# Clearing the padding rows of two sorted token tables chunk by chunk in the attention stages instead of at the start of the expert stages

## The chip, the cores and the metric

The kernel runs on one core of a Trainium2 chip. The metric is the time of one execution in microseconds of device time; three runs of the kernel before are given. The profile is of one further execution. Engines are named as in the profile: PE (matrix products), DVE (vector), ACT (activations), POOL (GpSimd) and SP (which here only issues transfers).

## What is computed

The reference is a two-layer model on x of shape 16 x 512 x 128 (16 sequences, here called chunks, of 512 tokens, width 128), float32. Each of its four parts is followed by a residual sum and a layer norm:

```python
x = layernorm(x + L0_attn(x))   # 16 heads of 64, exponentials of k1, k2, k3 products, cumulative sums over the tokens
x = layernorm(x + L0_ffn(x))    # 8 experts, each token goes to one: relu(x W1 + b1) W2 + b2, times its probability
x = layernorm(x + L1_attn(x))   # softmax attention, 16 heads of 8, with a bias that depends on the distance
x = layernorm(x + L1_ffn(x))    # a shared gated block plus one of 8 gated experts per token, token scaled by a score
```

Which expert a token goes to is the argmax of its 8 routing logits.

## The kernel before

The program has five stages with a barrier of all engines between them (`program`, L1898): the first attention (`attention_one`, L168), the first experts (`experts`, L826, tag b), the second attention (`attention_two`, L1083, tiles named c_), the second experts (`experts`, tag d) and `finish` (L1717, tiles named e_). Within a stage each engine has its own program, and semaphores order them.

**The sorted tables.** While an attention stage runs, it also routes: for each token of a chunk it chooses the expert and a slot, which is the next free row in that expert's region of a table in HBM, and POOL scatters the token rows there by an indirect DMA, four DMAs of 128 rows a chunk. The table is `xs_d` in the first attention (`route_scatter`, L628) and `zs_d` in the second (`scatter`, L1303). It has eight regions of REGION = 16 x 512 + 512 = 8,704 rows of 512 bytes, and behind them, from row SPARE on, one group of 512 spare rows. Before the scatter of chunk b, at most 512 b tokens have been given out, so every slot of chunk b is below row 512 (b + 1) of its region.

**The experts.** The expert stage works through 24 blocks of 512 rows (GROUP). Each expert's tokens are rounded up to whole blocks, so the last block of an expert has rows behind the last token, and blocks that no expert needs read the spare rows. These padding rows are computed like others and must hold finite numbers; nobody reads what comes of them. At the stage's start DVE works out a plan from the counts (L942 to L980): the expert of each block (`expert`, L964, signalled as `plan_ready` 1) and the first row of each block (`row`, L980, `plan_ready` 2), and behind that the rows for the later gather (L986 to L999). The padding is cleared at the same time: POOL sets a tile of zeros (L933) and one of ones (L934, for which the plan's first instruction waits), DVE converts each expert's end to an integer (`fill`, L940), and SP and ACT each load four of the eight ends into a register and issue a DMA of 512 rows of zeros from there on (`fill_behind`, L898); SP also clears the spare rows (L905). Only then does SP wait for the plan, load expert and row into registers (`which`), wait for all nine fills, and issue the first block's tokens (L919) and weights (L920). In the blocks PE transposes the tokens (L1060), ACT copies them out of PSUM, PE multiplies (L1052, L1073) and DVE writes the output tile.

**The order of SP's work in the first attention.** SP's program is a software pipeline over chunks, written out by hand in `step`: at step s it loads the turned x of chunk s + 1 (`load_turned`, L281, once the values of chunk s - 1 are through), the token-wise x of chunk s (`load`, L286, once `y_read` counts s - 1), and stores the normed rows of chunk s - 2 (L291). PE wants the turned x of chunk s + 1 in the middle of step s (`front_logits`, L360 and L363). All this goes through one queue. In step 0 SP also writes the table of position biases to HBM, in step 2 it loads all of it into SBUF:

```python
                    if isinstance(s.b, int) and s.b == 2:
                        sp.wait_ge(sem("bias_out"), 16 * H)
                        sp.dma_start(keep.bias[:], io["bias_d"].rearrange("h p d q -> p h d q")
```

The write is 16 DMAs of 448 KB (L308), the load is one DMA of 7,168 KB (L319). POOL's step ends with the scatter of chunk s - 3; behind it stand the next step's one-hot, rstd and running sums.

**SP in the second attention.** For each chunk SP writes the three bf16 parts of q and k to HBM (`parts_d`, L1240), waits for them and loads them back stacked in six DMAs (`c_kst`, `c_qst`, L1251), loads x1 of a later chunk (L1233) and stores x3 of the chunk before (L1256). A body of PE is 64 tiles: scores (L1348), the turned exponentials (L1357) and the values (L1370). The scores of the next chunk start six tiles before the body's end.

Of the kernel before, what the change touches and what calls it, by code (L numbers as in the profile page):

```python
# [14 lines left out]
I32 = mybir.dt.int32  # L15
# [4 lines left out]
P = 128  # L20
# [146 lines left out]

def attention_one(nc, g, keep):  # L168
# [9 lines left out]
    with ExitStack() as ctx:  # L178
# [91 lines left out]
        with nc.Block() as block:  # L270

            @block.sync
            def _(sp):
# [36 lines left out]
                def step(s, on):  # L310
                    if on[0]:
                        load_turned(s.ahead())
                    if on[1]:
                        load(s)
                    if isinstance(s.b, int) and s.b == 0:
                        make_bias()
                    if isinstance(s.b, int) and s.b == 2:
                        sp.wait_ge(sem("bias_out"), 16 * H)
                        sp.dma_start(keep.bias[:], io["bias_d"].rearrange("h p d q -> p h d q")  # L319
                                     ).then_inc(sem("bias_ready"), 16)  # L320
                    if on[3]:
                        store(s.back(2))

                loop(sp, step, first=0)
                sp.wait_ge(sem("bias_ready"), 16)
# [229 lines left out]
            def _(pool):  # L555
# [68 lines left out]
                def route_scatter(s):  # L624
                    pool.wait_ge(sem("slot_ready"), s.b + 1)
                    apart(pool, sem("pool_passed"))
                    for t in range(T):
                        pool.indirect_dma_start(  # L628
                            out=io["xs_d"], out_offset=bass.IndirectOffsetOnAxis(ap=slot[s.par][:, t:t + 1], axis=0),
                            in_=x1[s.par][:, t, :], in_offset=None).then_inc(sem(f"scat{s.par}"), 16)  # L630
# [195 lines left out]
def experts(nc, g, keep, tag, src, dst, weights, gated):  # L826
# [17 lines left out]
    with ExitStack() as ctx:  # L844
# [6 lines left out]
        zeros = sb("zeros", [P, T, W])  # L851
# [6 lines left out]
        fill = sb("fill", [P, E], I32)  # L858
# [33 lines left out]
        def fill_behind(eng, experts):  # L892

            eng.wait_ge(sem("zeros_ready"), 1)
            eng.wait_ge(sem("fill_ready"), 1)
            for e in experts:
                r = which(eng, fill, e, SPARE - GROUP)
                eng.dma_start(rows_of(src, r), zeros[:]).then_inc(sem("fill_out"), 16)  # L898

        with nc.Block() as block:  # L900

            @block.sync
            def _(sp):
                fill_behind(sp, range(0, E, 2))
                sp.dma_start(rows_of(src, SPARE), zeros[:]).then_inc(sem("fill_out"), 16)  # L905
                sp.wait_ge(sem("plan_ready"), 1)

                def step(s, on):
                    if on[0]:
# [4 lines left out]
                        if isinstance(s.b, int) and s.b == 0:  # L914
                            sp.wait_ge(sem("fill_out"), 16 * E + 16)
# [15 lines left out]
            @block.gpsimd  # L931
            def _(pool):
                nc.gpsimd.memset(zeros[:], 0.0).then_inc(sem("zeros_ready"), 1)  # L933
                nc.gpsimd.memset(ones8[:], 1.0).then_inc(sem("ones8_ready"), 1)  # L934

            @block.vector
            def _(dve):
                v = nc.vector
                own = Own(dve, sem("own"), sem("dve_passed"))
                v.tensor_copy(fill[:], keep.run[:]).then_inc(sem("fill_ready"), 1)  # L940
# [82 lines left out]
            def _(act):  # L1023
                fill_behind(act, range(1, E, 2))

# [57 lines left out]
def attention_two(nc, g, keep):  # L1083
# [36 lines left out]
    with ExitStack() as ctx:  # L1120
# [103 lines left out]
        with nc.Block() as block:  # L1224

            @block.sync
            def _(sp):
# [31 lines left out]
                def body(s, tail=True, front=True):  # L1259
                    if front:  # L1260
                        stack(s.ahead())
                        if not isinstance(s.b, int) or s.b + 2 < NB:
                            load(s.ahead().ahead())
# [5 lines left out]
                load(at(1))  # L1269
                body(at(0), tail=False)  # L1270
# [7 lines left out]
                sp.wait_ge(sem("x3_out"), 16 * NB)  # L1278

            @block.gpsimd  # L1280
            def _(pool):
# [17 lines left out]
                def scatter(s):  # L1299
                    pool.wait_ge(sem("slot_ready"), s.b + 1)  # L1300
                    apart(pool, sem("pool_passed"))
# [645 lines left out]
def _layout(**a):  # L1947
# [33 lines left out]
    out["pos"] = np.broadcast_to(n, (P, N))  # L1981
    rows = np.arange(H * SP_).reshape(-1, P)
# [36 lines left out]
```

## Time and profile before

| | |
|---|---|
| three runs | 2399.13, 2405.56, 2406.78 us; median 2405.56 |
| the profiled execution | 2405.52 us, span from the first to the last instruction 2403.7 us |
| mean granted TensorE clock | 0.937 |
| busy share of the span | PE 84%, DVE 68%, ACT 64%, POOL 33% |
| DMA | 83,432 packets, 164.19 MB, mean 68 GB/s |
| of it SP's queue (q1) | 73,844 packets, 142.35 MB, 18.7% of 16 engines' span |

By the timeline the stages begin near 0, 630, 746, 2109 and 2265 us. Times in the profile are from the span's start. A row of the timeline gives start, duration, engine, line, operation, the tile written and the tiles read, a count where several instructions are merged (the duration is then from the first start to the last end), and in brackets how long the engine had been idle before it and what released it. SPq, ACTq and POOLq are the sequencers, where DMAs are issued: the duration there is that of the issue, not of the transfer.

### The profile page before, as it was taken

What the parts mean: (1) busy time and instruction counts of PE and PEld (TensorE: products, weight loads), DVE (VectorE), ACT (ScalarE), POOL (GpSimd) and SP (SyncE); (2) the same over time, 40 slices, a digit from 0 to 9 for tenths busy, and PEclk for the clock granted to TensorE, in tenths of its full rate; (3) what the DMA queues carried; (4) which work ended last, traced back from release to release, by engine and by line L of the source; (5) the groups of instructions that cost most, each with busy time, mean ns of one, the idle gap of its engine ahead of it and who ended that gap; (6) DMA issues with size and microseconds to landing.
All of it is one profiled execution on the core that took longest, in us unless ns stands there. A gap on an engine that the chain in (4) does not pass through costs nothing. (4 is left out here: it accounts for less than half of the span.)

```text
span 2403.7 us, 49686 instructions
## 1 busy us (share of the span) xinstructions
PE 2024.0 (84%) x14348; PEld 1303.3 (54%) x14348; DVE 1641.9 (68%) x4787; ACT 1534.9 (64%) x3427; POOL 796.7 (33%) x806
## 2 busy tenths in 40 slices
PE   8488878887394699999999999999999999669886
PEld 5256555656273455555555555555555555446553
DVE  6377888787212578878887788787877787533266
ACT  3355655554141688888888888888888888523221
POOL 4467888787101211221122122212220220100166
PEclk9788989899696799999999999999999999879999
DMA  2331110100363202210221022102210220044332
GB/s 73 113 141 35 33 35 32 34 28 30 121 214 114 65 25 65 72 54 26 66 71 54 21 71 72 48 26 72 72 46 28 72 62 7 11 162 164 117 97 88
DMA packets 83432, 164.19 MB, mean 68 GB/s; under 512 B 11428, under 2 KB 39076, under 8 KB 80884
## 3 DMA queue, kind: packets, MB, share of 16 engines
q1 hardware_dynamic: 73844, 142.35, 18.7%
q0 software_dynamic: 8192, 16.79, 2.3%
q8 instruction: 116, 1.90, 0.3%
q10 hardware_dynamic: 1152, 2.10, 0.2%
q14 instruction: 128, 1.05, 0.1%
HBM read 110.23 MB, written 58.31 MB: 70 GB/s over the span
## 5 line engine op out<-in xcount | busy, mean ns | idle before, releaser
L1610 DVE CUSTOM_DVE_ANT_0 c_sums<-c_s,bias 128x512 f32<-128x512 f32 x1024 | 671.9, 686 | 183.1 <-PE c_s L1348 143.7
L1498 ACT ACTIVATE c_sums<-c_sums,c_low 128x512 f32<-128x512 f32 x1024 | 735.3, 743 | 40.0 <-DVE c_low L1610 28.9
L1357 PE MATMUL c_turned<-ident,c_sums 128*128 128x128 f32 x4096 | 635.9, 278 | 28.9 <-ACT c_pT L1205 27.9
L1357 PEld LDWEIGHTS c_turned<-ident,c_sums 128*128 128x128 f32 x4096 | 499.5, 143 | 180.4 <-ACT c_pT L1205 92.2
L1205 ACT COPY c_pT<-c_turned 128x512 f32<-128x512 f32 x768 | 455.6, 593 | 130.1 <-PE c_turned L1357 128.9
L1348 PE MATMUL c_s<-c_kst,c_qst 72*128 72x512 bf16 x1024 | 399.4, 391 | 46.5 <-DMA c_qst<-parts_d 28.2
L1370 PE MATMUL c_o<-c_pT,c_vst 128*32 128x256 f32 x4096 | 328.6, 393 | 0.7 <-ACT c_pT L1205 0.7
L1297 POOL TENSOR_TENSOR c_rstd<-c_ve,minus_half 128x4 f32<-128x4 f32 x32 | 32.9, 1029 | 639.4 <-DVE c_ve L122 639.4
L1205 DVE COPY c_pT<-c_turned 128x512 f32<-128x512 f32 x256 | 176.6, 690 | 87.3 <-PE c_turned L1357 85.1
L1348 PEld LDWEIGHTS c_s<-c_kst,c_qst 72*128 72x128 bf16 x1024 | 102.4, 100 | 233.3 <-issue 125.7
L505 ACT ACTIVATE v<-a_bank,gain 128x64 f32<-128x64 f32 x768 | 166.3, 345 | 55.5 <-DVE vp L718 55.4
L371 PE MATMUL a_bank<-wv,xT 128*128 128x512 f32 x256 | 153.5, 685 | 19.9 <-ACT v L505 15.2
L513 ACT COPY oT<-a_bank 128x512 f32<-128x512 f32 x128 | 69.7, 587 | 148.7 <-PE a_bank L392 148.6
L572 POOL TENSOR_TENSOR q<-q,vp 128x1024 f32<-128x1024 f32 x48 | 122.8, 2558 | 107.3 <-DVE vp L718 107.1
L583 POOL TENSOR_TENSOR s<-q,v 128x1024 f32<-128x1024 f32 x48 | 143.1, 2980 | 0.2
L400 PEld LDWEIGHTS a_bank<-wo,oT 128*128 128x128 f32 x1024 | 130.2, 203 | 14.3 <-issue 14.3
L718 DVE TENSOR_TENSOR vp<-a_bank,ez 128x512 f32<-128x512 f32 x96 | 64.8, 687 | 104.3 <-PE a_bank L371 102.6
L1303 POOL DMA_INDIRECT zs_d<-c_xs,c_slot x64 | 62.9, 982 | 217.4 <-DVE c_slot L1666 200.8
L400 PE MATMUL a_bank<-wo,oT 128*128 128x128 f32 x1024 | 132.4, 286 | 0.0
L1370 PEld LDWEIGHTS c_o<-c_pT,c_vst 128*32 128x32 f32 x4096 | 81.3, 108 | 87.6 <-issue 86.1
L734 DVE TENSOR_TENSOR o<-o,r 128x1024 f32<-128x1024 f32 x64 | 127.9, 2018 | 0.0
L392 PE MATMUL a_bank<-ident,o 128*128 128x128 f32 x512 | 81.6, 310 | 54.2 <-DVE o L734 53.4
(252 smaller groups left out, 2788.9 us busy)
## 6 DMA issues: line engine op xcount, KB each, us to landing
c_kst<-parts_d SPq DMA_DIRECT2D x48, 384.0 KB
c_qst<-parts_d SPq DMA_DIRECT2D x48, 384.0 KB
parts_d<-c_parts SPq DMA_DIRECT2D x32, 384.0 KB, 2.5
d_w<-in_wd SPq DMA_DIRECT2D x24, 384.0 KB, 3.2
b_w<-in_wb SPq DMA_DIRECT2D x24, 321.0 KB, 3.3
bias_d<-line_d SPq DMA_DIRECT2D x16, 448.0 KB
bias<-bias_d SPq DMA_DIRECT2D x1, 7168.0 KB, 21.9
b_x<-xs_d SPq DMA_DIRECT2D x24, 256.0 KB, 2.5
```

Of the source, the lines that this page charges most:

```text
L371: nc.tensor.matmul(v_ps[h][:], xT[s.par][:, t, :], wv[:, 512 * h:512 * h + 512], start=True, stop=True).then_inc(sem("v_ready"), 1)
L400: mm = nc.tensor.matmul(y_ps[:, t * W:(t + 1) * W], oT[t % 2][:, k, :], wo[:, k, :], start=(k == 0), stop=(k == HA // P - 1))
L505: ins = nc.scalar.activation(dst[:, h * A:(h + 1) * A], v_ps[half][:, k * A:(k + 1) * A], ACT.Copy, scale=gain[s.par][:, t, h:h + 1])
L572: nc.gpsimd.tensor_tensor(q[:, t, :], q[:, t - 1, :], vp[t % 2][:], ALU.add).then_inc(sem("q_ready"), 1)
L583: nc.gpsimd.tensor_tensor(s1[s.par][:, t, :], q[:, t - 1, :], v2[t % 2][:], ALU.add).then_inc(sem("s1_ready"), 1)
L734: v.tensor_tensor(heads(o[t % 2][:]), heads(o[t % 2][:]), r[s.par][:, t, :].unsqueeze(2).to_broadcast([P, H, A]), ALU.mult).then_inc(sem(" ...
L1205: engine(pT[r % 2][:, :, m // 2, m % 2 * P:(m % 2 + 1) * P], pT_ps[m % 2][:]).then_inc(sem(copied(s, n)[0]), 1)
L1348: nc.tensor.matmul(s_ps[n % BANKS][:], qst[s.par][:, h, t * P:(t + 1) * P], kst[s.par][:, h, :], start=True, stop=True).then_inc(sem("s_ps ...
L1357: mm = nc.tensor.transpose(pT_ps[n % 2][:, c, :], sums[n % BUFS][:, c * P:(c + 1) * P], keep.ident[:])
L1370: mm = nc.tensor.matmul(o_ps[ARRAY * i:ARRAY * (i + 1), r % 2 * 2 * P:(r % 2 + 1) * 2 * P], vst[s.par][:, c, f:f + ARRAY], pT[r % 2][:, c, ...
L1498: nc.scalar.activation(sums[b][:], sums[b][:], ACT.Exp, bias=low[b][:], scale=-1.0).then_inc(sem("exp_done"), 1)
L1610: v.tensor_tensor_reduce(sums[n % BUFS][:], s_ps[n % BANKS][:], bias, 1.0, 3.0e38, ALU.add, ALU.min, low[n % BUFS][:]).then_inc(sem("low_r ...
```

## The change

Two helpers are added. `clear_rows` is a DMA from a new input of zeros (128 x 2,048 bytes in HBM) to rows 512 b to 512 b + 511 of all eight regions; `clear_spare` clears the spare rows. SP issues `clear_spare` once and one `clear_rows` per chunk in each attention stage: in the first behind the token-wise load of step b, in the second at the start of body b, that is behind the store that ends the body before. POOL's scatter of chunk b first waits until the clears 0 to b have landed, and SP waits for all of them at the stage's end. The first 16 of each region's 17 groups are cleared. In the expert stages the zeros tile, the integer ends, the nine fills and the waits for them are gone. The whole diff (no other line differs):

```diff
@@ -163,6 +163,17 @@
     own.wait()
     own.did(v.tensor_reduce(slotf[:], sel[:], AX, ALU.add))
     own.wait()
+
+
+def clear_rows(eng, name, b, io, done):
+
+    regions = io[name][0:SPARE, :].rearrange("(e r) w -> e r w", e=E)
+    eng.dma_start(regions[:, bass.ds(GROUP * b, GROUP), :].rearrange("e (p t) w -> p e (t w)", t=T),
+                  io["zeros"].unsqueeze(1).to_broadcast([P, E, T * W])).then_inc(done, 16)
+
+
+def clear_spare(eng, name, io, done):
+    eng.dma_start(io[name][bass.ds(SPARE, GROUP), :].rearrange("(p t) w -> p (t w)", t=T), io["zeros"]).then_inc(done, 16)
 
 
 def attention_one(nc, g, keep):
@@ -312,6 +323,7 @@
                         load_turned(s.ahead())
                     if on[1]:
                         load(s)
+                        clear_rows(sp, "xs_d", s.b, io, sem("rows_clear"))
                     if isinstance(s.b, int) and s.b == 0:
                         make_bias()
                     if isinstance(s.b, int) and s.b == 2:
@@ -321,7 +333,10 @@
                     if on[3]:
                         store(s.back(2))
 
+                clear_spare(sp, "xs_d", io, sem("spare_clear"))
                 loop(sp, step, first=0)
+                sp.wait_ge(sem("spare_clear"), 16)
+                sp.wait_ge(sem("rows_clear"), 16 * NB)
                 sp.wait_ge(sem("bias_ready"), 16)
                 sp.wait_ge(sem("x1_out0"), 16 * NB // 2)
                 sp.wait_ge(sem("x1_out1"), 16 * NB // 2)
@@ -623,6 +638,7 @@
 
                 def route_scatter(s):
                     pool.wait_ge(sem("slot_ready"), s.b + 1)
+                    pool.wait_ge(sem("rows_clear"), 16 * (s.b + 1))
                     apart(pool, sem("pool_passed"))
                     for t in range(T):
                         pool.indirect_dma_start(
@@ -848,14 +864,12 @@
         bank = [ctx.enter_context(nc.psum_tensor(f"{tag}_bank{i}", [P, GROUP], F32)) for i in range(8)]
         turn_ps, gate_ps, h_ps = bank[0:2], bank[2:4], bank[4:6]
         y_ps = [b[:].rearrange("p (t w) -> p t w", t=T) for b in bank[6:8]]
-        zeros = sb("zeros", [P, T, W])
         count = sb("count", [P, E])
         blocks = sb("blocks", [P, E])
         ones8 = sb("ones8", [P, E])
         ends = sb("ends", [P, E])
         offs = sb("offs", [P, E])
         first = sb("first", [P, E])
-        fill = sb("fill", [P, E], I32)
         past = sb("past", [P, BLOCKS, E])
         ef = sb("ef", [P, BLOCKS])
         isf = sb("isf", [P, BLOCKS, E])
@@ -889,20 +903,10 @@
         def rows_of(name, first):
             return io[name][bass.ds(first, GROUP), :].rearrange("(p t) w -> p t w", t=T)
 
-        def fill_behind(eng, experts):
-
-            eng.wait_ge(sem("zeros_ready"), 1)
-            eng.wait_ge(sem("fill_ready"), 1)
-            for e in experts:
-                r = which(eng, fill, e, SPARE - GROUP)
-                eng.dma_start(rows_of(src, r), zeros[:]).then_inc(sem("fill_out"), 16)
-
         with nc.Block() as block:
 
             @block.sync
             def _(sp):
-                fill_behind(sp, range(0, E, 2))
-                sp.dma_start(rows_of(src, SPARE), zeros[:]).then_inc(sem("fill_out"), 16)
                 sp.wait_ge(sem("plan_ready"), 1)
 
                 def step(s, on):
@@ -911,8 +915,6 @@
                         if isinstance(s.b, int) and s.b == 0:
                             sp.wait_ge(sem("plan_ready"), 2)
                         r = which(sp, row, s.b, SPARE)
-                        if isinstance(s.b, int) and s.b == 0:
-                            sp.wait_ge(sem("fill_out"), 16 * E + 16)
                         need(sp, sem("y_ps"), s.b - 3)
                         if not gated:
                             need(sp, sem("y_ready"), s.b - 3)
@@ -930,14 +932,12 @@
 
             @block.gpsimd
             def _(pool):
-                nc.gpsimd.memset(zeros[:], 0.0).then_inc(sem("zeros_ready"), 1)
                 nc.gpsimd.memset(ones8[:], 1.0).then_inc(sem("ones8_ready"), 1)
 
             @block.vector
             def _(dve):
                 v = nc.vector
                 own = Own(dve, sem("own"), sem("dve_passed"))
-                v.tensor_copy(fill[:], keep.run[:]).then_inc(sem("fill_ready"), 1)
                 dve.wait_ge(sem("ones8_ready"), 1)
                 own.did(v.tensor_scalar(offs[:], keep.iota[:], float(REGION), None, ALU.mult))
                 own.did(v.tensor_scalar(first[:], keep.iota[:], float(REGION), None, ALU.mult))
@@ -1021,8 +1021,6 @@
 
             @block.scalar
             def _(act):
-                fill_behind(act, range(1, E, 2))
-
                 def step(s, on):
                     if on[0]:
                         act.wait_ge(sem("turn_ps"), s.b + 1)
@@ -1257,6 +1255,7 @@
                                  ).then_inc(sem("x3_out"), 16)
 
                 def body(s, tail=True, front=True):
+                    clear_rows(sp, "zs_d", s.b, io, sem("rows_clear"))
                     if front:
                         stack(s.ahead())
                         if not isinstance(s.b, int) or s.b + 2 < NB:
@@ -1267,6 +1266,7 @@
                 load(at(0))
                 stack(at(0))
                 load(at(1))
+                clear_spare(sp, "zs_d", io, sem("spare_clear"))
                 body(at(0), tail=False)
                 with sp.Fori(0, NB // 2 - 2) as i:
                     for s in steps(i, 2):
@@ -1276,6 +1276,8 @@
                 body(at(NB - 1), front=False)
                 store(at(NB - 1))
                 sp.wait_ge(sem("x3_out"), 16 * NB)
+                sp.wait_ge(sem("spare_clear"), 16)
+                sp.wait_ge(sem("rows_clear"), 16 * NB)
 
             @block.gpsimd
             def _(pool):
@@ -1298,6 +1300,7 @@
 
                 def scatter(s):
                     pool.wait_ge(sem("slot_ready"), s.b + 1)
+                    pool.wait_ge(sem("rows_clear"), 16 * (s.b + 1))
                     apart(pool, sem("pool_passed"))
                     for t in range(T):
                         pool.indirect_dma_start(
@@ -1979,6 +1982,7 @@
     }
     n = np.linspace(0.0, 1.0, N, dtype=f).reshape(P, T).T.reshape(N)
     out["pos"] = np.broadcast_to(n, (P, N))
+    out["zeros"] = np.zeros((P, T * W), f)
     rows = np.arange(H * SP_).reshape(-1, P)
     out["hmask"] = (rows.T[:, :, None] // SP_ == np.arange(H)).astype(f)
     out["ident"] = np.eye(P, dtype=f)
```

## Rows read from the trace of the kernel before

**Rows 1.** The page's first line.

```profile
span 2403.7 us, 49686 instructions
```

**Rows 2.** Windows, both attentions: start:end, length, busy us of each engine, PEclk, DMA share, GB/s.

```profile
48.00:630.00 582.00, 431.48 (x2331) 309.68 (x2330) 414.61 (x898) 303.34 (x1200) 416.77 (x385) 0.88 0.16 53
...
745.00:2109.00 1364.00, 1220.40 (x10176) 740.11 (x10176) 1033.09 (x3417) 1104.74 (x2016) 267.48 (x298) 0.96 0.17 51
```

**Rows 3.** Timeline at the start of the first expert stage, all engines.

```profile
629.88 0.53 POOL L933 MEMSET b_zeros<- 128x512 f32 x1 [7.92 <-POOLq L1913]
629.92 0.51 DVE L940 CAST b_fill<-run 128x8 int32<-128x8 f32 x1 [13.58 <-PEq L1913]
630.35 0.13 POOL L934 MEMSET b_ones<- 128x8 f32 x1
630.51 0.17 DVE L942 TENSOR_SCALAR b_offs<-iota 128x8 f32<-128x8 f32 x1
...
631.53 4.24 SPq L898 DMA_DIRECT2D xs_d<-b_zeros  x4
...
632.67 0.18 DVE L964 TENSOR_SCALAR b_expert<-b_ef 128x24 int32<-128x24 f32 x1
...
634.64 0.18 DVE L980 TENSOR_TENSOR b_row<-b_rowf,b_spare 128x24 int32<-128x24 f32 x1
...
635.81 0.44 SPq L905 DMA_DIRECT2D xs_d<-b_zeros  x1
...
638.71 0.23 DVE L999 TENSOR_TENSOR rows<-slots,b_chosen 128x64 uint32<-128x64 f32 x1
639.21 0.36 SPq L919 DMA_DIRECT2D b_x<-xs_d  x1
...
641.66 1.12 PE L1060 MATMUL b_bank<-ident,b_x 128*128 128x128 f32 x4 [27.09 <-DMA b_x<-xs_d]
```

**Rows 4.** Timeline at the start of the second expert stage.

```profile
2113.80 0.18 DVE L980 TENSOR_TENSOR d_row<-d_rowf,d_spare 128x24 int32<-128x24 f32 x1
...
2118.37 0.35 SPq L919 DMA_DIRECT2D d_x<-zs_d  x1
```

**Rows 5.** Windows: writing the bias table, loading it, the tail of the first stack.

```profile
70.00:80.00 10.00, 6.43 (x11) 2.53 (x10) 4.85 (x7) 5.89 (x28) 5.44 (x3) 0.74 0.50 152
...
148.00:158.00 10.00, 7.60 (x52) 6.01 (x51) 8.47 (x19) 3.90 (x12) 5.79 (x3) 0.96 1.03 403
...
784.00:786.00 2.00, 0.00 (x0) 0.00 (x0) 0.00 (x0) 0.00 (x0) 0.00 (x0) 0.50 0.17 74
```

**Rows 6.** Timeline of SP in the first attention, steps 2 to 4.

```profile
115.55 0.33 SPq L281 DMA_DIRECT2D xT<-in_xT  x1
...
137.51 0.44 SPq L319 DMA_DIRECT2D bias<-bias_d  x1
...
148.91 0.33 SPq L281 DMA_DIRECT2D xT<-in_xT  x1
170.64 0.33 SPq L286 DMA_DIRECT2D xtok<-in_x  x1
...
182.71 0.33 SPq L281 DMA_DIRECT2D xT<-in_xT  x1
```

**Rows 7.** Timeline of PE: the logits of chunk 4 in step 3.

```profile
167.28 0.49 PE L360 MATMUL a_bank<-p,ident 128*128 128x192 f32 x2
```

**Rows 8.** Line L281 between 100 and 200 us: issue to landing of its three DMAs.

```profile
DMA to landing us min/median/max: 2.6/2.6/11.8
```

**Rows 9.** Who waited for whom: in total, times, longest.

```profile
PE c_s L1348 <- DMA c_qst<-parts_d: 28.2, 1, 28.2
```

**Rows 10.** Timeline of SP in the second attention, behind the first stack.

```profile
775.21 0.42 SPq L1233 DMA_DIRECT2D c_x<-x_d  x1
```

**Rows 11.** Windows: end of the second stack (all engines), and score matmuls alone.

```profile
854.00:858.00 4.00, 4.00 (x38) 2.47 (x37) 3.83 (x11) 3.00 (x6) 0.00 (x0) 1.00 0.03 11
...
796.00:870.00 74.00, 26.68 (x65) 0.93 0.18 52
```

## The prediction

> **What bounds the kernel now.** I read the time stage by stage, because the edit touches four of the five stages in different ways. The profiled execution has a span of 2403.7 us [rows 1] and a time of 2405.52 us; the median of the three runs is 2405.56 us, so the sum below, made against 2405.5, holds for the median too. The runs spread over 7.65 us (2399.13 to 2406.78), 0.3% of the time; under that a measurement of this kernel can hardly tell a change from none.
>
> First the windows by stage [rows 2]. In the first attention PE is busy 431 of 582 us and DVE and POOL some 415 each: three engines close together, DMA share 0.16. In the second attention PE is busy 1220 of 1364 us with DMA share 0.17. Neither stage is bound by transfers, so work given to the DMA engines there has room on average, and the question is where a transfer is waited for.
>
> Then the timeline where the first expert stage begins [rows 3]. PE starts its first transpose at 641.66, released by the DMA of the first token block, which SP issued at 639.21. Everything from 629.9 to 641.7 is start-up on one chain. Two things run side by side in it: DVE's plan, whose last wanted result (the row numbers) is written at 634.64 + 0.18 = 634.82, and SP's clearing of the padding, four fills in 4.24 us and one more, ended at 636.25, then two value loads and a short wait. SP, not the plan, sets the start. The other expert stage has the same picture: plan written at 2113.98, first token DMA at 2118.37 [rows 4].
>
> **Removed: the fills in both expert stages.** Three pieces lie on the path.
>
> (a) POOL's memset of the zeros tile (0.53 us) stands ahead of the memset of ones for which DVE's plan waits. Without it the ones are ready at 629.88 + 0.13 = 630.01 and DVE can start at 630.04 (it started 0.03 us after the ones before), not 630.51: 0.47 us. The first DVE instruction took 0.51 us where like ones take 0.17, so 0.34 of it could be a cost of starting that now falls on the plan. I take 0.40, between 0.1 and 0.47.
>
> (b) SP's issue. The cost of one value load: the fill table is ready at 629.92 + 0.51 = 630.43, and SP's first fill starts at 631.53, 1.10 us later. From the four fills: (4.24 - 0.33) / 3 = 1.30 us from one to the next, less 0.33 of issue, 0.97 us. After the change SP loads the expert number at 632.85 (plan, part one [rows 3]), is done with it by 634.0, waits for part two at 634.82 - 0.40 = 634.42, loads the row number in 1.10 us and issues the first token DMA at 635.52. Before it was 639.21: 3.69 us gained. In the other stage: 2113.98 - 0.40 + 1.10 = 2114.68 against 2118.37, 3.69 us.
>
> (c) ACT's four fills run beside SP's, long before the first transpose, for which ACT waits; and the first tokens took 2.45 us from issue to PE behind nine fills of 256 KB, so their traffic held nothing up: nothing.
>
> Behind the first token DMA everything keeps its spacing: weights, second block, PE. What is late next is still SP's two value loads; DVE's remaining plan, which ended at 638.94, ends near 638.5, and the first block needs DVE only behind transpose, copy and first product, later than 640. So the whole stage moves: -7.4 us for both. Bounds: if both value loads only start after part two, (639.21 - 634.72 - 2.20) = 2.3 each, -4.6; with 0.97 and 0.47, 3.9 each, -7.8.
>
> **Added: 16 clears in each attention.** One clears 512 rows in each of eight regions, 8 x 512 x 512 B = 2.10 MB, in 1,024 pieces of 2 KB, HBM to HBM. No row of before has just that. The nearest one is the writing of the bias table from line_d, also HBM to HBM, in 512 B pieces: 152 GB/s at a DMA share of 0.50 [rows 5]. The fastest is the loading of the bias, 403 GB/s at a share of 1.03. So a clear lasts 2.10/0.403 = 5.2 us at best, 13.8 us if 152 GB/s is all that HBM to HBM gives, and 152/0.50 = 304 GB/s, 6.9 us, if a full share scales. I take 6.9: its row is the same kind of copy, and the clear's pieces are larger. The Trainium skill ("DMA: Bandwidth & Descriptors", section "Why a DMA increments its semaphore by 16 and not by 1") says that the slowest dimensions of the two patterns set the number of engines; by it the clear, with 128 outermost, has all 16 and the sum keeps 6.9, not 13.8. The trace agrees so far: the bias table is written with 7 outermost, and its share of 0.50 is near 7/16.
>
> Most clears are covered. In the first attention SP issues one after the token load, as at 170.97, and its next urgent DMA is the turned x at 182.71 [rows 6]: 11.7 us of room, and a turned x is wanted only 18 us after its issue (148.91 to 167.28 for chunk 4, [rows 7]). Steps of 33.4 us (115.55 to 148.91, with 20 us of full DMA in it) and 33.8 us (to 182.71, with almost none) show that full DMA engines alone don't slow the step. Clears 0 and 1 stand on the queue behind the last DMA that PE waits for there.
>
> **One place isn't covered**: chunk 2. There the clear goes onto SP's queue at 137.5, ahead of the 7 MB bias load, and the turned x of chunk 4 is issued behind that at 148.91. It landed 11.8 us later [rows 8], at 160.7, and PE wanted it at 167.28. The room is 6.6 us. A clear of 6.9 us uses it up: +0.3 us; 5.2 us costs nothing; 13.8 us costs 7.2.
>
> The second attention: the stack transfers are waited for once, 28.2 us at its start [rows 9]. The first clear is issued behind them (SP issued the load behind them at 775.21 [rows 10]), so in ring order it can't hold them up; while their tail runs at 74 GB/s on a share of 0.17, most engines are idle and take the clear. Later stacks have ended by 858, and the 65th score matmul, the first that wants the new stack, comes just before 870 [rows 11]: 12 us of room against a clear issued behind the stack. Nothing.
>
> **Waits.** POOL's scatter now waits for the clears up to its chunk; behind it on POOL stand the next step's rstd and running sums, for which DVE and ACT wait. But clear b is issued three steps (100 us) before scatter b in the first attention, a whole body of 64 tiles ahead in the second. What stays is the instruction: 32 times some 0.03 us, at most 1 us; I take 0.5. The waits of SP at the ends are for clears issued long before.
>
> Sum: 2405.5 - 7.4 + 0.3 + 0.5 = **2398.9 us**.
>
> **Rivals.** *A smaller gain.* SP's start is only partly freed (both value loads behind the plan), -4.6, or a start pays back a few tenths here and there: 2405.5 - 4.6 + 0.8 = 2401.7 us. For it: the plan ends only 1.4 us before the last fill. Against: the expert number is ready 2 us ahead of the row numbers.
>
> *A slow clear ahead of the bias load; slower.* The writes of one clear jump between eight regions 4.25 MiB apart; should that run at the tail's 74 GB/s [rows 5], a clear lasts 28 us, the turned x of chunk 4 lands 21.7 us late for PE, and the time is 2405.5 - 7.4 + 21.7 + 0.5 = 2420 us; each step's turned x would then be at the edge too. It decides from a clear of 13.5 us on, where the stall eats the 7 us gained. For it: no row has such a stride. Against: 304 to 403 GB/s wherever enough engines were busy. The Trainium skill (same page, section on latency and other measured facts) tells of HBM copies with a row pitch of 4 MiB at 103 GB/s and 214 when padded off the power of two. By 103 a clear would last 20 us and the time be near 2412; by 214, 9.8 us and 2402. No run here shows either.
>
> **How the numbers follow.** Forecast as worked out 0.55, a smaller gain or a few us back at chunk 4 0.35, slow clear 0.10. The line of 0.3% is at 2398.3, right beside my 2398.9, and the run spread of 7.65 us lies across it: of the first case somewhat over half comes out faster than that line, the second mostly within it. Faster 0.41, same 0.50, slower 0.09. Range: best sum 2397.7 less half the spread, 2394; upward the smaller gain, a clear of up to 11 us and the spread, 2406.
>
> **Right or wrong in the profile after.** The first token DMA 5.6 us after POOL's first memset in the expert stages, not 9.3; first transpose 2.5 us behind; the fills gone. In the first attention PE's logits of chunk 4 without a DMA wait over 1 us, and the turned x of chunk 4 landing by 168. The wait for the first stack still about 28 us. DMA share in the stages up by 16 x 6.9 us. A wait of POOL's scatter for a clear, or a DMA wait at those logits above 7 us, would prove me wrong.

## The result, and the profile after

The changed kernel takes 2393.03 us (median of 16 runs, 2387.75 to 2400.82), the kernel before 2402.47 us in 16 runs beside it (2398.38 to 2406.78). The ratio is 0.9963, 95% interval 0.9954 to 0.9973: faster by 6.5 to 11 us. The forecast was 2398.9 us with a range of 2394 to 2406, so the time fell 1 us below the range. About half of the 5.9 us between forecast and time is the level, the time of the kernel before from which the forecast subtracts: the kernel before, which I had at 2405.5 us from three runs and one profile, is at 2402.5 us in sixteen.

The profiled execution took 2393.4 us. First the timeline where the expert stages begin, against [rows 3, 4]:

```profile
626.63 0.10 POOL L935 MEMSET b_ones<- 128x8 f32 x1 [7.93 <-POOLq L1916]
626.77 0.17 DVE L942 TENSOR_SCALAR b_offs<-iota 128x8 f32<-128x8 f32 x1 [13.70 <-POOL b_ones L935]
...
628.93 0.18 DVE L964 TENSOR_SCALAR b_expert<-b_ef 128x24 int32<-128x24 f32 x1
...
630.91 0.18 DVE L980 TENSOR_TENSOR b_row<-b_rowf,b_spare 128x24 int32<-128x24 f32 x1
...
631.87 0.36 SPq L921 DMA_DIRECT2D b_x<-xs_d  x1
...
634.58 1.12 PE L1058 MATMUL b_bank<-ident,b_x 128*128 128x128 f32 x4 [23.28 <-DMA b_x<-xs_d]
...
2100.68 0.10 POOL L935 MEMSET d_ones<- 128x8 f32 x1 [3.80 <-POOLq L1916]
...
2104.96 0.18 DVE L980 TENSOR_TENSOR d_row<-d_rowf,d_spare 128x24 int32<-128x24 f32 x1
...
2105.93 0.35 SPq L921 DMA_DIRECT2D d_x<-zs_d  x1
...
2108.44 1.11 PE L1058 MATMUL d_bank<-ident,d_x 128*128 128x128 f32 x4 [19.51 <-DMA d_x<-zs_d]
```

Read each stage from POOL's first memset, since the start itself moves: the first attention was 3.2 us shorter in this execution. To the first token DMA it is 631.87 - 626.63 = 5.24 us, where it was 639.21 - 629.88 = 9.33: 4.09 us gained. In the other stage it is 5.25 us, where it was 2118.37 - 2109.05 = 9.32; the memset of before stands at

```profile
2109.05 0.53 POOL L933 MEMSET d_zeros<- 128x512 f32 x1 [3.83 <-POOLq L1913]
```

The row numbers are ready at 631.09 and SP issues 0.78 us later; the plan, no longer the fills, sets the start.

Then SP's queue in steps 2 and 3 of the first attention, against [rows 6]; PE's logits of chunk 4, against [rows 7]; and the bias load's time to landing from the page (it was 21.9 us):

```profile
137.24 0.33 SPq L297 DMA_DIRECT2D xtok<-in_x  x1
137.61 0.62 SPq L171 DMA_DIRECT2D xs_d<-in_zeros  x1
138.28 0.67 SPq L331 DMA_DIRECT2D bias<-bias_d  x1
147.38 6.91 SPq L302 DMA_DIRECT2D x_d<-x  x1
154.33 1.09 SPq L292 DMA_DIRECT2D xT<-in_xT  x1
170.76 0.33 SPq L297 DMA_DIRECT2D xtok<-in_x  x1
171.13 0.59 SPq L171 DMA_DIRECT2D xs_d<-in_zeros  x1
```

```profile
168.09 0.59 PE L375 MATMUL a_bank<-p,ident 128*128 128x192 f32 x2 [0.53 <-DMA xT<-in_xT]
```

```profile
bias<-bias_d SPq DMA_DIRECT2D x1, 7168.0 KB, 28.5
```

The clear ahead of it made the bias load land 6.6 us later, and PE waits 0.53 us for the turned x: the one uncovered place, near the forecast size of 0.3. The turned x landed 13.7 us behind its issue, at 168.0, at the edge of what I had said; no wait of POOL's scatter for a clear is in the trace. SP's issue of the x1 store took 6.91 us there, of which below.

Last, windows over both attentions [rows 2] and over the clear of chunk 0, and the wait for the first stack [rows 9]:

```profile
48.00:626.60 578.60, 427.77 (x2331) 306.44 (x2330) 413.04 (x897) 301.95 (x1200) 417.42 (x384) 0.89 0.32 108
738.00:2100.00 1362.00, 1218.30 (x10176) 738.68 (x10176) 1034.72 (x3417) 1103.75 (x2016) 266.92 (x298) 0.96 0.24 76
...
17.00:20.00 3.00, 3.00 (x14) 2.84 (x15) 2.93 (x5) 1.26 (x2) 2.27 (x3) 1.00 1.03 401
```

```profile
PE c_s L1351 <- DMA c_qst<-parts_d: 27.5, 1, 27.5
```

DMA share rose from 0.16 to 0.32 and from 0.17 to 0.24, no engine's busy time changed by as much as 1%, and the first stack is waited for as before. From 17 to 20 us, where the kernel before moved nothing, the clear of chunk 0 runs alone at 401 GB/s. The Trainium skill ("DMA: Bandwidth & Descriptors", section "Latency and other measured facts") gives 214 GB/s as the full rate of its HBM-to-HBM copies, and 103 at a pitch of 4 MiB; with regions 4.25 MiB apart this trace shows neither. By the Trainium skill (same page, section "Why a DMA increments its semaphore by 16 and not by 1") the clear uses 16 engines, and the share of 1.03 agrees.

### The profile page after: what moved, and what is told of

The parts are those of the page before. It is cut to its first block and busy times, and to the rows that moved or that the text cites. A ratio compares the mean times of both kernels' runs of the same rounds, so it can differ in the third digit from the quotient of the medians.

```text
span 2391.6 us, 49680 instructions
## 1 busy us (share of the span) xinstructions
PE 2020.0 (84%) x14348; PEld 1300.1 (54%) x14348; DVE 1641.1 (69%) x4785; ACT 1533.0 (64%) x3427; POOL 797.4 (33%) x804
## 5 line engine op out<-in xcount | busy, mean ns | idle before, releaser
L587 POOL TENSOR_TENSOR q<-q,vp 128x1024 f32<-128x1024 f32 x48 | 124.9, 2602 | 104.4 <-DVE vp L734 104.0
L598 POOL TENSOR_TENSOR s<-q,v 128x1024 f32<-128x1024 f32 x48 | 142.9, 2978 | 0.1
L415 PEld LDWEIGHTS a_bank<-wo,oT 128*128 128x128 f32 x1024 | 127.3, 200 | 14.3 <-issue 14.3
L415 PE MATMUL a_bank<-wo,oT 128*128 128x128 f32 x1024 | 129.6, 282 | 0.0
L750 DVE TENSOR_TENSOR o<-o,r 128x1024 f32<-128x1024 f32 x64 | 123.6, 1951 | 0.0
```

Of the source, the lines that this page charges most:

```text
L415: mm = nc.tensor.matmul(y_ps[:, t * W:(t + 1) * W], oT[t % 2][:, k, :], wo[:, k, :], start=(k == 0), stop=(k == HA // P - 1))
L587: nc.gpsimd.tensor_tensor(q[:, t, :], q[:, t - 1, :], vp[t % 2][:], ALU.add).then_inc(sem("q_ready"), 1)
L598: nc.gpsimd.tensor_tensor(s1[s.par][:, t, :], q[:, t - 1, :], v2[t % 2][:], ALU.add).then_inc(sem("s1_ready"), 1)
L750: v.tensor_tensor(heads(o[t % 2][:]), heads(o[t % 2][:]), r[s.par][:, t, :].unsqueeze(2).to_broadcast([P, H, A]), ALU.mult).then_inc(sem(" ...
```

## The experiments

Eighteen experiments in five groups. Each group ran on one chip beside its own runs of the kernel before; ratios are against those. In the expectations "changed kernel" is the one after, and a group is a "call". The diffs show the lines that matter; waits and declarations that go with them are left out.

**Group 1: which part gives, which costs.** The kernel before took longer here than in the first measurement (2420.1 us). `e1_both` adds the clears and keeps the fills:

```diff
                         load(s)
+                        clear_rows(sp, "xs_d", s.b, io, sem("rows_clear"))
...
                 def body(s, tail=True, front=True):
+                    clear_rows(sp, "zs_d", s.b, io, sem("rows_clear"))
```

> The clears and their waits are added to the two attention stages, and the nine fills stay in the expert stages (work is done twice, nothing is left out). My theory: the whole gain of the change lies at the two starts of the expert stages, and the 3.2 us by which the first attention was shorter in the profile after is spread between executions; then this kernel is within 1 us of before, on the slow side (0.5 us at chunk 4's logits, little else), and from POOL's first memset in an expert stage to SP's first token DMA it is 9.3 us as before. Rival A: the clears shorten the first attention, whatever the reason; then it is some 3 us faster than before. Rival B: each clear costs a few tenths, hidden so far behind the spread; then it is 3 to 6 us slower.

Measured: 0.9994 (0.9980 to 1.0008), and 9.32 us from memset to token DMA as before. The interval is -4.8 to +1.9 us, so rival B, 3 to 6 us slower, is out. My theory of no difference fits; rival A lies inside the interval too, and this run alone doesn't exclude it.

`e2_few` takes the fills away and nearly all clears with them:

```diff
-                        clear_rows(sp, "xs_d", s.b, io, sem("rows_clear"))
...
+LAST = {"xs_d": (2, 0, 4, 1, 4, 0, 0, 1), "zs_d": (1, 1, 1, 2, 1, 2, 2, 2)}
...
 def clear_spare(eng, name, io, done):
+    for e, k in enumerate(LAST[name]):
+        first = e * REGION + k * GROUP
+        eng.dma_start(io[name][bass.ds(first, GROUP), :].rearrange("(p t) w -> p (t w)", t=T), io["zeros"]).then_inc(done, 16)
```

> The fills are gone as in the changed kernel, but in place of 16 clears of all regions each attention clears once, at its start, the spare rows and one group of 512 rows in each region, the one in which the last token of this data falls (it leaves out the other clears, 15/16 of the traffic). My theory: the removal alone is worth 8 us, so this is at 2394 to 2395 us and within 1 us of the changed kernel, ahead of it by the 0.5 us at chunk 4. Rival A (the clears shorten the first attention): 3 us slower than the changed kernel. Rival B (the clears cost): 3 to 6 us faster than it, 2388 to 2391.

Measured: 0.9961 (0.9937 to 0.9984), that is 4 to 15 us faster. The changed kernel didn't run in this group, so this run alone doesn't price the clears: it excludes neither rival. What bears on it is the same kernel beside the changed one in groups 3 and 4, and the stages in the table below.

`e3_ones_first` swaps two lines in the kernel before:

```diff
-                nc.gpsimd.memset(zeros[:], 0.0).then_inc(sem("zeros_ready"), 1)
                 nc.gpsimd.memset(ones8[:], 1.0).then_inc(sem("ones8_ready"), 1)
+                nc.gpsimd.memset(zeros[:], 0.0).then_inc(sem("zeros_ready"), 1)
```

> The kernel before with POOL's two memsets in the other order, ones ahead of zeros. My theory: DVE's plan is done 0.4 to 0.5 us earlier, its first instruction costs 0.17 us and not 0.5, and the time stays as it is, since SP's fills and not the plan set the start: first token DMA still 9.3 to 9.5 us behind the first memset. Rival: the plan sets it, and the first token DMA comes 0.4 us earlier, 0.8 us over both stages.

Measured: 0.9991 (0.9973 to 1.0009). Its timeline:

```profile
635.96 0.10 POOL L933 MEMSET b_ones<- 128x8 f32 x1 [7.93 <-POOLq L1913]
636.00 0.53 POOL L934 MEMSET b_zeros<- 128x512 f32 x1
636.10 0.47 DVE L942 TENSOR_SCALAR b_offs<-iota 128x8 f32<-128x8 f32 x1
...
640.48 0.18 DVE L980 TENSOR_TENSOR b_row<-b_rowf,b_spare 128x24 int32<-128x24 f32 x1
...
645.33 0.36 SPq L919 DMA_DIRECT2D b_x<-xs_d  x1
```

The token DMA stays 9.37 us behind the first memset though the plan ends 0.24 us earlier: before, the fills set the start. The expectation on DVE's first instruction was wrong. It takes 0.47 us here, beside POOL's memset of zeros, and 0.17 us in the changed kernel, where that memset is gone. So the 0.34 us that I had feared as a cost of starting goes with running beside the memset.

`e4_control` is the kernel before:

> The kernel before, unchanged, for the spread of its stages between executions. My theory (the 3.2 us of the first attention are spread): the time from the start to POOL's first memset of the expert stage (629.9 us in the profile before) moves by 2 us or more between this execution and the other three of this call, whose first attentions differ from it by nothing or by the clears alone. Rival: it stays within 0.5 us of 629.9, and the 3.2 us have a cause.

Measured: 0.9999 (0.9983 to 1.0015). POOL's first memset came at 639.67 here, 635.96 in e3, whose first attention has the same instructions, 641.16 in e2 and 642.42 in e1. That is 3.7 us between two executions with the same instructions, so 3.2 us need no cause.

**Group 2: the uncovered place, doubled clears, a better order.** Before: 2485.15 us on this chip, 65 to 84 us more than in the other groups. `e5_again` is the changed kernel.

> The changed kernel, unchanged, for comparison within this call and as a second execution of its stages. My theory: 8 to 9 us faster than before (0.9966 to 0.9963); from POOL's first memset to SP's first token DMA 5.2 us in both expert stages against 9.3 before; the wait of chunk 4's logits for the turned x again 0.5 us; the first attention's length differs from before's by spread of either sign. Rival (the clears shorten the first attention): it is some 3 us shorter than before's again.

Measured: 0.9996 (0.9983 to 1.0010): no gain where I expected 8 to 9 us; by the interval at most 4. The memset-to-DMA time is 5.25 us as it should be, the wait at chunk 4 is 1.4 us. `e6_four_at_chunk2` and `e7_twice` add clears of tables that nobody reads: the middle lines of the diff are e6's, three more at chunk 2; the last is e7's, one more at every chunk, and likewise of vs_d in the second attention:

```diff
                         clear_rows(sp, "xs_d", s.b, io, sem("rows_clear"))
+                        if isinstance(s.b, int) and s.b == 2:
+                            for k in range(3):
+                                clear_rows(sp, "ws_d", k, io, sem("extra_clear"))
...
+                        clear_rows(sp, "ws_d", s.b, io, sem("extra_clear"))
```

> The changed kernel with three more clears, of a table that nobody reads, behind the clear of chunk 2 and so ahead of the bias load. My theory: a clear lasts 5.3 to 6 us, the turned x of chunk 4 lands 16 to 18 us later, the wait of PE's logits for it grows from 0.5 to 16.5 to 18.5 us, and all of it comes back in the time: 16 to 18 us slower than the changed kernel. Rival: the stage has slack between its engines that takes up a good part, and the time grows by 10 us or less.

> The changed kernel with every clear doubled: behind each one a clear of the same size of another table that nobody reads, in both attentions (32 clears more, 67 MB). My theory: the cost is at chunk 4 alone, 5.3 to 6 us more wait there, and the rest stays hidden: 5 to 6 us slower than the changed kernel, DMA share of the first attention 0.32 before, some 0.48 here. Rival (the clears cost a little everywhere, and the changed kernel's 0.2 us each is lost in the spread): 11 to 13 us slower. Third: in the second attention the stacks are held up, which a DMA wait of the scores (L1351 there) for c_qst in more than one place would show.

The wait at chunk 4 in e6, then in e7, then in e5:

```profile
PE a_bank L379 <- DMA xT<-in_xT: 21.4, 1, 21.4
```

```profile
PE a_bank L377 <- DMA xT<-in_xT: 8.5, 1, 8.5
```

```profile
PE a_bank L375 <- DMA xT<-in_xT: 1.4, 1, 1.4
```

So a clear ahead of the bias load costs (21.4 - 1.4) / 3 = 6.7 us and 7.1 us, a little above what I expected of these runs and on the 6.9 of the prediction. e6 is at 1.0087 (1.0073 to 1.0102), 0.0091 or 22.6 us over e5; its first attention is 648.46 - 626.09 = 22.4 us longer. The wait of 20 us comes through whole as far as the intervals (some 5 us) can tell; slack that takes up half of it, the rival, is out. e7 is at 1.0034 (1.0021 to 1.0046), 9.4 us over e5 with 7.1 of wait: 67 MB more of clears cost 2.3 us besides, which the intervals don't tell from nothing. They don't exclude the rival's 11 to 13 us either. The scores waited for c_qst once, 27.7 us, so the third is out.

`e8_order` moves two things on SP's queue in the changed kernel: the clear of chunk 2 goes behind the bias load, the store and the turned x instead of ahead of them, and the first expert's weights are loaded ahead of the wait for the plan:

```diff
+                    if isinstance(s.b, int) and s.b == 2:
+                        load_turned(at(4))
+                        clear_rows(sp, "xs_d", s.b, io, sem("rows_clear"))
...
                         e = which(sp, expert, s.b, E - 1)
                         if isinstance(s.b, int) and s.b == 0:
+                            weights_in(s, e)
                             sp.wait_ge(sem("plan_ready"), 2)
```

> The changed kernel with two shifts on SP's queue: at chunk 2 the bias load and the turned x of chunk 4 go out ahead of the clear, and in the expert stages the weights of block 0 are issued as soon as its expert is known, ahead of the wait for the row numbers, so that the second block's tokens go out 0.5 us earlier. My theory: no DMA wait at chunk 4's logits; second token DMA 1.7 us behind the first and not 2.2; 1 to 1.5 us faster than the changed kernel, which the times can hardly show. Rival: the start of the blocks is bound elsewhere (the weights, or the copy of the turned tokens), and only the 0.5 us of chunk 4 is won.

Measured: 0.9995 (0.9983 to 1.0007); read with e16 below.

**Groups 3 and 4: the slow chip or the change?** I had no profile of the kernel before on the chip of group 2. The changed kernel's profile there (the second line; the first is that of the first measurement) shows a second attention with a lower granted clock, 0.95 for 0.98, and fewer instructions done in the same stretch. Its bodies, the 64 tiles of one chunk, took 85 and 90 us, elsewhere 79 and 83; below I call them long and short:

```profile
840.00:2090.00 1250.00, 1164.30 (x9812) 707.93 (x9810) 986.22 (x3274) 1058.89 (x1932) 240.43 (x267) 0.98 0.23 73
```

```profile
840.00:2090.00 1250.00, 1140.88 (x9199) 687.88 (x9199) 930.26 (x3060) 1004.52 (x1822) 234.90 (x261) 0.95 0.23 73
```

> The kernel before, unchanged, beside the changed one on one chip. The call before ran on a chip on which every kernel took 80 us more, nearly all of it in the second attention (bodies of 85 and 90 us for 79 and 83), and there the change gained nothing (0.9996). Where the chip of this call has such long bodies: by my theory the bodies of this kernel are as long as the changed one's, within 0.3 us on average; by the rival (there the clears cost about what the fills gave) they are 0.5 us shorter, 8 us over the stage. On a chip with bodies of 79 and 83 us both say: equal bodies, within 0.1 us.

> The changed kernel beside the control. On a chip with bodies of 79 and 83 us in the second attention: 8 to 9 us faster than before, 0.9966 to 0.9963. On one with bodies of 85 and 90 us: by my theory that the ratio of 0.9996 was chance or came from the first attention, 0.997 or lower; by the rival, 0.999 to 1.000 again.

`e11_first_table` applies the change to xs_d and leaves zs_d as before (`if gated:` around the fills, no clears in `attention_two`):

> The change for the first table alone: clears in the first attention, no fills in the first expert stage; the second attention and the second expert stage are as before. My theory: each expert start gives 4.1 us, so this is 4 us faster than before (0.9983 to 0.9985), on any chip. Rival (the clears of the second attention cost on a chip with long bodies): there this kernel too is 4 us faster, while the changed kernel with both is not faster at all.

> The fills gone, and in place of the clears by chunk one group of 512 rows in each region and the spare rows at the start of each attention (it leaves out 15/16 of the clearing). On a chip with bodies of 79 and 83 us in the second attention: as the changed kernel, within 1 us. On one with bodies of 85 and 90 us: by my theory as the changed kernel too; by the rival (the clears cost there) some 8 us faster than it.

Measured, on a chip with short bodies (before: 2411.62 us): e9 1.0002 (0.9987 to 1.0017), e10 0.9970 (0.9954 to 0.9985), e11 0.9977 (0.9961 to 0.9993), e12 0.9977 (0.9960 to 0.9993). Half the change gives 5.5 us where I said 4, the whole 7.2, few clears 5.5: all fit 4 us per table within their intervals, and no finer order among the three can be read. Few clears (e12) are not faster than all of them (e10).

> The changed kernel again. On a chip with bodies of 79 and 83 us in the second attention: 0.9963 to 0.9972 of before. On one with 85 and 90 us: by my theory (the clears cost nothing there either) 0.997 or lower, by the rival (the clears cost 8 us there) 0.999 to 1.000.

> The kernel before, unchanged, for the length of its stages on the same chip: 1.000 within its interval. Second attention from its first weight load to the next stage's first memset within 1.5 us of the changed kernel's by my theory, some 8 us shorter than it by the rival where the bodies are long.

> The fills gone and 15/16 of the clears left out. My theory: as the changed kernel, within 1 us plus the 0.5 to 1.4 us of chunk 4's wait, on any chip. Rival: 8 us faster than the changed kernel where the bodies are long.

Measured, again with short bodies (before: 2401.36 us): e13 0.9957 (0.9945 to 0.9969), e14 1.0000 (0.9991 to 1.0009), e15 0.9966 (0.9953 to 0.9979). Again few clears (e15) win nothing over all of them (e13).

**Group 5.** Before: 2414.87 us, short bodies.

> The changed kernel with the bias load and chunk 4's turned x ahead of the clear at chunk 2, and block 0's weights ahead of the row numbers. My theory: no DMA wait at chunk 4's logits (0.5 to 1.4 us won), first transposes of the second block 0.5 us nearer to the first's in both expert stages: 1 to 2 us faster than the changed kernel, 0.995 to 0.9965 of before on a chip with bodies of 79 and 83 us. Rival: the blocks are bound elsewhere and nothing over 0.5 us is won.

> The changed kernel once more. With bodies of 79 and 83 us: 0.9957 to 0.997. With 85 and 90 us: 0.997 or lower by my theory, 0.999 to 1.000 by the rival.

> The kernel before, unchanged: 1.000 within its interval. With bodies of 85 and 90 us in the changed kernel, this one's are as long by my theory and 0.5 us shorter on average by the rival.

Measured: e16 0.9953 (0.9930 to 0.9975), e17 0.9961 (0.9945 to 0.9978), e18 0.9983 (0.9966 to 1.0001). That the unchanged kernel comes out at 0.9983 says how far a ratio of this group can stray. The record gives the granted clock of each run. The control's twelve had 0.9348 on average and came out 4.2 us shorter (of means) than the runs of before beside them at 0.9314; e17's twelve had 0.9347 and came out 8.7 us shorter. So some 4 us of e17's gain are what the kernel before also shows at that clock, and 4.5 us are left for the change. In e16's trace both shifts work: no DMA wait at chunk 4, and from the memset to the first product it is 10.43 us, where the changed kernel had 637.62 - 626.63 = 10.99:

```profile
640.09 0.10 POOL L944 MEMSET b_ones<- 128x8 f32 x1 [7.93 <-POOLq L1925]
...
643.62 0.36 SPq L917 DMA_DIRECT2D b_w<-in_wb  x1
645.32 1.99 SPq L930 DMA_DIRECT2D b_x<-xs_d  x2
...
650.52 3.62 PE L1059 MATMUL b_bank<-b_xT,b_w 128*128 128x512 f32 x4
```

It may be 1 us faster than the changed kernel; the times don't show it, here or in e8.

**The stages over all executions.** From the profiles with short bodies, in us. "Experts b" is from POOL's first memset to SP's first weight load of the second attention, and holds the column before it; "experts d and finish" is from that stage's first memset to the end:

| | first attention, to the memset | memset to token DMA | experts b | second attention | experts d and finish |
|---|---|---|---|---|---|
| before (6 executions: before, e3, e4, e9, e14, e18), mean | 634.7 | 9.34 | 116.3 | 1362.8 | 294.5 |
| their range | 625.4 to 639.9 | 9.33 to 9.37 | 115.9 to 117.2 | 1362.0 to 1363.3 | 293.1 to 295.7 |
| after (4: after, e10, e13, e17), mean | 636.4 | 5.24 | 112.7 | 1363.1 | 291.1 |
| their range | 624.1 to 648.6 | 5.24 | 112.2 to 113.6 | 1361.6 to 1364.2 | 289.7 to 292.1 |
| few clears (3: e2, e12, e15), mean | 638.0 | 5.22 | 112.5 | 1363.5 | 291.0 |
| clears and fills (e1) | 642.4 | 9.32 | 115.9 | 1364.3 | 296.4 |

The expert stages give 3.6 and 3.5 us before rounding, 7.1 together; the second attention costs 0.3, inside its spread. Few clears and all of them agree within 0.4 us in every stage but the first. (In e1, one execution, the last two stages are 1.5 and 1.9 us above the means of before.) The first attention drowns everything; without it the execution is 1773.6 us before and 1766.8 after, 6.8 less.

## Why the prediction was right or wrong

**What bounds the start of the expert stages: right.** SP's fills set it (e3 moved the plan and not the start), and the plan sets it now.

**Part (a), the memset: right, sized low.** Memset to row numbers fell from 4.94 to 4.46 us, 0.48 for my 0.40; I had held back for a cost of starting that e3 shows to be the memset's own.

**Part (b), the value load: the term that was mis-sized.** I took 1.10 us from the ready table to the DMA, from the fills. It was 0.78 (631.87 - 631.09). With the 0.08 us more of part (a) that makes 4.09 us per start for my 3.69, 8.2 for 7.4.

**"So the whole stage moves": right within the spread.** Of the 4.09 us the stages kept 3.6 and 3.5 in the means. The rest is not told from nothing: from the token DMA to SP's next weight load it took 106.5 to 107.9 us in the six executions and 106.9 to 108.3 in the four. The longest of these, e10, has one cause in its trace: the second token block was waited for, and its transposes came 3.7 us behind the first, 2.1 to 2.3 in the other three. The start gave more than I said and the stages perhaps kept less, 7.1 us against my 7.4.

**Covered clears: right** (the table; e10 with e12, e13 with e15). **Chunk 4: right**, with 0.5 to 1.5 us of wait in five executions of the changed kernel and one of e1 where I said 0.3 (and in two of them above the 1 us that I had set as a sign), a clear of 6.7 to 7.1 us (e6, e7) where I said 6.9, and the wait passed on whole (e6). The rate that a clear has alone, 401 GB/s, would have been too low a price there. **The slow clear: refuted.** **A smaller gain: not what happened** in the starts, which gave 4.09 us each for its 2.3.

**The number and the range: wrong.** The step that failed is the level, in "2405.5 - 7.4 + 0.3 + 0.5" and again in "best sum 2397.7 less half the spread". It came from a median of three and one profile, both near the top of what the kernel does, and the range left no room for that. Sixteen runs put it at 2402.5 us, 3.0 lower. With 2402.5 the same working gives 2395.9 us, and 2391 as the lower end, and the measured 2393.03 lies inside. (The upper end doesn't come out of its terms either: the smaller gain and a clear of 11 us make 2405.8 already, so 2406 holds no spread.)

The other 2.8 us are gain, 9.4 for my 6.6, and only in part a term that was too small. The starts gave 8.2 for 7.4; the traces outside the first attention show 6.8 less, and the wait at chunk 4 takes 0.5 to 1.5 of it back, which leaves 5.3 to 6.3, a little below my 6.6. The measured ratios on the chips with short bodies, 0.9963, 0.9970, 0.9957 and 0.9961, stand for 7.2 to 10.3 us. Where the rest comes from isn't shown. In group 5 some 4 us go with a higher granted clock that the control had too; for the first measurement no clocks of the runs of before are on record. That the clears shorten the first attention by a few us, rival A of e1, is not excluded: single executions of it differ by 24 us in the same kernel, so the means of four and six of them say nothing at this size.

**Open.** On the chip of group 2 the change gained nothing in time, though its token DMA came as early as elsewhere. e5 and e8 agree on it. No profile of the kernel before was taken on such a chip, so what took the gain isn't settled. That the clears cost 8 us there in the second attention is unlikely: e7 has them doubled, and its second attention is 4.3 us longer than e5's and 0.9 shorter than that of e8, which has as many as e5.

## What to carry to other kernels

Work of a stage start that doesn't depend on the stage before's result (here: zeros for rows that may stay empty) can go into a compute-bound stage as bulk DMA: here 67 MB cost 0.5 to 1.5 us that the traces show, where 4.7 MB at a barrier had cost 7 to 8. In this kernel the price lay only where the same queue next carried something big that is waited for, so look for the one chunk with an irregular transfer. And before forecasting a change of 0.3%, put a level and a spread on the baseline that more than three runs support.

## What the runs showed of the hardware

**The first attention varies by 24 us from execution to execution.** The same kernel (e10 and e13) took 648.6 and 624.1 us for it, and the other executions lie in between; its steps are 34.0 us each in the one and mostly 31 to 32 in the other. Two things differ in the line groups, with the same number of instructions: DVE's product L750, and PE's products, of which L415 is one. First e10, then e13:

```profile
L750 DVE TENSOR_TENSOR o<-o,r 128x1024 f32<-128x1024 f32 x64 | 144.8, 2281 | 0.0
...
L415 PE MATMUL a_bank<-wo,oT 128*128 128x128 f32 x1024 | 136.9, 292 | 0.0
```

```profile
L415 PE MATMUL a_bank<-wo,oT 128*128 128x128 f32 x1024 | 127.6, 279 | 0.0
...
L750 DVE TENSOR_TENSOR o<-o,r 128x1024 f32<-128x1024 f32 x64 | 124.3, 1961 | 0.0
```

The mean granted clock up to the memset was 0.85 in e10 and 0.90 in e13, between TensorE's two levels of 1.2 and 2.4 GHz (0.5 and 1.0). Over the executions on record a longer first attention has, on the whole, the lower clock and the longer L750. Which is the cause and which follows was not separated.

**DVE and POOL hold each other up.** L750 takes 1.21 us at best and up to 3.4. Two places of one step of e10:

```profile
405.44 1.34 DVE L750 TENSOR_TENSOR o<-o,r 128x1024 f32<-128x1024 f32 x1
405.65 3.35 POOL L598 TENSOR_TENSOR s<-q,v 128x1024 f32<-128x1024 f32 x1
...
410.56 2.34 POOL L587 TENSOR_TENSOR q<-q,vp 128x1024 f32<-128x1024 f32 x1 [0.42 <-DVE vp L734]
410.58 3.41 DVE L750 TENSOR_TENSOR o<-o,r 128x1024 f32<-128x1024 f32 x1
```

In each pair the one that starts second is the longer one: POOL's L598 takes 3.35 us here and 2.35 at 414.52, and DVE's L750 ends 1.1 us behind the end of POOL's L587. POOL's sums L587 go the other way on average (2,374 ns in e10, 2,602 ns in e13), so which of the two waits shifts between executions.

**SP's issue of a DMA can take microseconds.** Behind a clear and the bias load the issue of a 256 KB store took 6.91 us (0.35 before, 7.47 in e13, 18.76 in e6 with four clears ahead), and the turned x was issued 5.4 us later for it. I read it as a queue that is full; no run shows the queue itself. It seems to have cost nothing: the turned x landed at 168.0, 1.2 us behind the bias load ahead of it. A wait on SP behind such an issue would have come later by as much.
